# A four-layer graph network: ScalarE takes the filter's first dense layer out of its PSUM bank, VectorE adds a turn later, the sort's transposes stand at the turn's end

## What is computed

```python
def ssp(x):
    return jax.nn.softplus(x) - LOG2
f = ssp(edge @ We1 + be1)
f = f @ We2 + be2
msg = xn[edge_index[1]] * f
agg = jax.ops.segment_sum(msg, edge_index[0], num_segments=N)
```

```python
e = jnp.exp(e - seg_max[dst])
denom = jax.ops.segment_sum(e, dst, num_segments=N)
out = jax.ops.segment_sum(h[src] * alpha[:, None], dst, num_segments=N)
```

## Time and profile before

| | us |
|---|---|
| median of 3 runs | 5322.7 |
| lowest, highest | 5319.41, 5327.09 |
| the profiled execution | 5334.7 |
| its span, first to last instruction | 5332.7 |

### The profile page before, as it was taken

How to read it: one execution, slowest core, us unless ns; L and a number is a source line. 1 busy time by engine, 2 the same in 40 slices (tenths; PEclk the granted TensorE clock), 3 DMA queues, 4 the chain that set the end, 5 groups by cost and what they waited for, 6 DMA issues and landing times. The chain is left out here.

```text
span 5332.7 us, 53511 instructions
## 1 busy us (share of the span) xinstructions
PE 2639.6 (49%) x13173; PEld 2222.8 (42%) x13173; DVE 2702.5 (51%) x7382; ACT 1319.8 (25%) x3951; POOL 3391.0 (64%) x3625
## 2 busy tenths in 40 slices
PE   1477777777566654444443544344443243334445
PEld 1355555556455553333333443333333133333333
DVE  2699888888766653333333443333333533333334
ACT  4587666667366650000000210000000000000001
POOL 0677666767222237777777557777777377777773
PEclk8799888889676775555555665555555555555556
DMA  4676666667388872222221122122222322222224
GB/s 74 175 172 167 149 154 152 159 154 171 54 256 256 261 220 53 53 53 53 53 53 52 38 62 53 51 52 53 53 53 52 51 53 53 51 52 53 53 53 50
DMA packets 460042, 516.96 MB, mean 97 GB/s; under 512 B 85627, under 2 KB 358863, under 8 KB 459734
## 3 DMA queue, kind: packets, MB, share of 16 engines
q0 software_dynamic: 131072, 301.89, 23.9%
q1 hardware_dynamic: 325780, 210.91, 14.4%
q10 hardware_dynamic: 2882, 0.70, 0.1%
HBM read 386.68 MB, written 126.50 MB: 96 GB/s over the span
## 5 line engine op out<-in xcount | busy, mean ns | idle before, releaser
L1476 PE MATMUL bank<-arena 128*128 128x128 f32 x4992 | 1277.0, 438 | 1951.7 <-DVE arena L873 1663.3
L1551 POOL DMA_INDIRECT arena<-node_table,pick x1664 | 1589.4, 955 | 650.8 <-issue 506.9
L1476 PEld LDWEIGHTS bank<-arena 128*128 128x128 f32 x4992 | 1111.3, 328 | 2117.1 <-DVE arena L873 1847.5
L861 DVE TENSOR_TENSOR acc<-acc,bank 128x128 f32 x2496 | 720.4, 289 | 2081.5 <-PE bank L1476 1790.8
L1551 POOL DMA_INDIRECT arena<-gat_table,pick x832 | 850.3, 1022 | 357.7 <-issue 235.0
L1551 POOL DMA_INDIRECT arena<-message_table,pick x832 | 788.7, 948 | 255.8 <-issue 253.2
L1169 ACT COPY xt<-bank 128x512 f32<-128x512 f32 (+1 forms) x39 | 21.6, 554 | 2115.2 <-PE bank L1428 2115.2
L873 DVE TENSOR_TENSOR arena<-iota_free,local 128x512 f32<-128x512 f32 x624 | 428.2, 687 | 3.8 <-issue 2.5
L1465 PE MATMUL bank<-arena 128*128 x1664 | 324.7, 367 | 202.6 <-DVE arena L902 198.6
L1465 PEld LDWEIGHTS bank<-arena 128*128 128x128 f32 x1664 | 293.0, 270 | 234.3 <-issue 233.4
L1630 POOL DMA_DIRECT2D message_table<-arena x208 | 112.8, 542 | 393.1 <-DVE arena L902 389.4
(11 more groups left out here) (215 smaller groups left out, 3167.7 us busy)
## 6 DMA issues: line engine op xcount, KB each, us to landing
arena<-filter_table SPq DMA_DIRECT2D x832, 64.0 KB, 3.2
message_table<-arena POOLq DMA_DIRECT2D x208, 256.0 KB, 3.5
filter_table<-arena SPq DMA_DIRECT2D x196, 256.0 KB
xt<-edge_cols SPq DMA_DIRECT2D x131, 256.0 KB, 3.0
arena<-local_rows SPq DMA_DIRECT2D x208, 128.0 KB
arena<-local_rows POOLq DMA_DIRECT2D x52, 512.0 KB, 5.9
arena<-node_table,pick POOLq DMA_INDIRECT x1664
arena<-edge_cols SPq DMA_DIRECT2D x65, 256.0 KB
```

What stands on the lines that cost most here:

```text
L861: e.tensor_tensor(a, a, bank[6 + t % 2][:, s * P:(s + 1) * P], ALU.add).then_inc(sums, 1)
L1476: ins = e.matmul(bank[6 + n % 2][:, s * P:(s + 1) * P], hot[n % 2][:, s, :], gathered[:, slot(n, s), 0:D], start=True, stop=True)
L1551: e.indirect_dma_start(out=dst, out_offset=None, in_=table, in_offset=bass.IndirectOffsetOnAxis(ap=index, axis=0)).then_inc(done, 16)
```

## The change

ScalarE now reads `bank[0]` twice, right after each other: Abs into `magn` as before, and Relu with the same bias into `edge_t[u % 4]`, the buffer from which the matmul has just read its edges. Then `bank[0]` is free (new semaphore f_taken), and f_hidden_of waits on that and no longer on f_plus. VectorE's f_plus_of becomes a sum of two SBUF tiles and moves one turn later, to lag 4, and from behind the weave to its last piece, so that it stands in the first round. f_filter and f_made_of follow at lags 5 and 6, the store at lag 7. The edge ring has four buffers, its load waits on f_plus. The softplus is split: f_front (Abs, Relu), then gat_weigh, then f_back (Exp, Ln).

The order within the turn changes too: on TensorE, ScalarE and SyncE the background now comes last and not first. A transposition takes two steps, one for each group of four transposes. A second background step comes each fourth turn. So the sort's list is 14 steps longer (238 in place of 224 on VectorE), and the seven window gathers move from GpSimd's turn 179 to 183. The rest are trims without a place in the loop: two rows of weights lie in the gather ring until the ring is used, one constant column, one semaphore and one wait are gone, the arena is larger.

```diff
 def background_turns(t):
-    return (1, 1 + (t % 5 == 0))
+    return (1, 1 + (t % 4 == 0))
...
             def f_plus_of(u):
                 e.wait_ge(f_log, u + 1)
-                e.scalar_tensor_tensor(magn[u % 2][:, :], bank[0][:, :], neg_col["L1_gnn_be1"][:, 0:1],
-                                       magn[u % 2][:, :], ALU.max, ALU.add).then_inc(f_plus, 1)
+                e.tensor_tensor(magn[u % 2][:, :], magn[u % 2][:, :], edge_t[u % 4][:, :], ALU.add).then_inc(f_plus, 1)
...
+                if 0 <= t - 4 < FTICKS:
+                    pieces.append(f_plus_of(t - 4))
                 weave(pieces, background, background_turns(t))
-                if 0 <= t - 3 < FTICKS:
-                    run(f_plus_of(t - 3))
...
+            def f_front(u):
+                e.wait_ge(f_hidden, u + 1)
+                if u > 1:
+                    e.wait_ge(f_done, u - 1)
+                own(e.activation(magn[u % 2][:, :], bank[0][:, :], ACT.Abs, bias=cols["L1_gnn_be1"][:, 0:1]))
+                e.activation(edge_t[u % 4][:, :], bank[0][:, :], ACT.Relu, bias=cols["L1_gnn_be1"][:, 0:1]
+                             ).then_inc(f_taken, 1)
+
+            def f_back(u):
+                m = magn[u % 2][:, :]
+                e.wait_ge(f_taken, u + 1)
+                q = own(e.activation(m, m, ACT.Exp, scale=-1.0))
+                e.wait_ge(own.sem, q)
+                e.activation(m, m, ACT.Ln, bias=1.0).then_inc(f_log, 1)
...
             for t in range(TICKS + 13):
-                weave([], background, background_turns(t))
+                for lag, fn in ((6, f_made_of), (3, f_front), (10, gat_weigh), (3, f_back)):
+                    if 0 <= t - lag < (TICKS if fn is gat_weigh else FTICKS):
+                        fn(t - lag)
                 for lag, fn in ((4, gat_dst), (9, gat_weight)):
                     if (t - lag) % GT == 0 and 0 <= t - lag < TICKS:
                         fn((t - lag) // GT)
-                for lag, fn in ((5, f_made_of), (10, gat_weigh), (3, f_soft)):
-                    if 0 <= t - lag < (TICKS if fn is gat_weigh else FTICKS):
-                        fn(t - lag)
+                weave([], background, background_turns(t))
...
             def f_hidden_of(u):
-                e.wait_ge(edge_in[u % 3], 16 * (u // 3 + 1))
+                e.wait_ge(edge_in[u % 4], 16 * (u // 4 + 1))
                 if u:
-                    e.wait_ge(f_plus, u)
+                    e.wait_ge(f_taken, u)
```

More of the change, by code:

```diff
@@ L171, in build_program @@
         mats = {name: sb("w_" + name, [P, D]) for name in MATS}
-        rows = {name: sb("r_" + name, [P, D]) for name in ROWS}
+        rows = {name: sb("r_" + name, [P, D]) for name in ROWS[2:]}
         cols = {name: sb("c_" + name, [P, 1]) for name in COLS}
@@ L252, in build_program @@
         gat_w, att_prod = gathered[:, 4, :], gathered[:, 5, 0:D]
+        rows.update({name: gathered[:, 6 + k, 0:D] for k, name in enumerate(ROWS[:2])})
         order_row, order_col, order_index, order_src = (
@@ L309, in build_program @@
         ring = [sem(f"ring{k}") for k in range(RT)]
-        sync_in = [sem(f"sync_in{k}") for k in range(6)]
-        edge_in, local_row_in, f_in = sync_in[0:3], sync_in[3:6], sync_in
-        f_hidden, f_log, f_plus, f_done, f_made = (
-            sem("filter_" + n) for n in ("hidden", "log", "plus", "done", "made"))
+        sync_in = [sem(f"sync_in{k}") for k in range(7)]
+        edge_in, local_row_in, f_in = sync_in[0:4], sync_in[4:7], sync_in[0:FT]
+        f_hidden, f_taken, f_log, f_plus, f_done, f_made = (
+            sem("filter_" + n) for n in ("hidden", "taken", "log", "plus", "done", "made"))
         f_out = [sem(f"filter_out{k}") for k in range(2)]
@@ L335, in build_program @@
                                      "x", "xturned", "xkept", "third", "rows"))
-        table_out = [sem(f"table{k}_out") for k in (1, 2)]
+        table_out = sem("table_out")
         plain_hot, plain_product, plain_summed = sem("plain_hot"), sem("plain_product"), sem("plain_summed")
@@ L590, in vector @@
                     e.sem_clear(f_log)
-                    e.scalar_tensor_tensor(magn[0][:, 0:P], bank[0][:, P:2 * P], neg_col["L1_gnn_be1"][:, 0:1],
-                                           magn[0][:, 0:P], ALU.max, ALU.add).then_inc(f_plus, 1)
+                    e.tensor_tensor(magn[0][:, 0:P], magn[0][:, 0:P], magn[1][:, 0:P], ALU.add).then_inc(f_plus, 1)
                     e.wait_ge(f_done, 1)
@@ L1019, in sort_keys @@
                             n += 1
+                            if not h:
+                                yield
                     cur = 1 - cur
@@ L1394, in f_hidden_of @@
             def f_hidden_of(u):
-                e.wait_ge(edge_in[u % 3], 16 * (u // 3 + 1))
+                e.wait_ge(edge_in[u % 4], 16 * (u // 4 + 1))
                 if u:
-                    e.wait_ge(f_plus, u)
-                e.matmul(bank[0][:, :], mats["L1_gnn_We1"][:, :], edge_t[u % 3][:, :], start=True, stop=True
+                    e.wait_ge(f_taken, u)
+                e.matmul(bank[0][:, :], mats["L1_gnn_We1"][:, :], edge_t[u % 4][:, :], start=True, stop=True
                          ).then_inc(f_hidden, 1)
@@ L1573, in second_list @@
                 for kind, _ in PLAN:
-                    if kind == "flip":
+                    if kind != "pair":
                         yield
@@ L1717, in sync @@
             background = [iter(()), second_list()]
-            for t in range(TICKS + 6):
-                weave([], background, background_turns(t))
+            for t in range(TICKS + 7):
                 if t < TICKS:
                     places_in(t)
-                if 0 <= t - 1 < FTICKS:
-                    edges_in(t - 1)
-                if 0 <= t - 6 < FTICKS:
-                    filters_out(t - 6)
+                if t < FTICKS:
+                    edges_in(t)
+                if 0 <= t - 7 < FTICKS:
+                    filters_out(t - 7)
+                weave([], background, background_turns(t))
             for g in background:
```

59 lines of the change are left out of this document (31 added, 28 removed).

## The result

The changed kernel takes 5447.24 us (median of 4 runs, 5434.27 to 5457.15); the kernel before, beside it, 5324.9 (4 runs, 5319.41 to 5338.7). The ratio is 1.0217, 95% interval 1.0196 to 1.0239. The prediction was 5262 with a range of 5235 to 5300, faster with a chance of 0.89. It was wrong in sign: 122 us were lost where 61 were to be gained. The profiled execution took 5457.15 us with a span of 5455.1, against 5334.7 and 5332.7, so the two traces, 122 us apart as well, show the whole difference.

A forecast was written before the change was run, and what follows sets the result against it. VectorE's work and waits were taken to bound the first layer, GpSimd closely behind. Earlier windows (-43), fewer turns of gathers (-20.6) and the tail (+2) gave -62, taken as -61: 5262 us, range 5235 to 5300.

The forecast's parts named there:

- Waits that go: VectorE's waits in the first layer for Ln, mask and a copy, 67.5 us, go, covered by slack between engines.
- the line on DMAs: SP's DMAs keep their count, are issued a turn ahead of use and hide under it; nothing counted for them.
- The rest: First layer's tail costs +2 us; SP's DMAs stay hidden; trims 0; everything behind the first layer moves as a block.
- What bounds the kernel before: First layer, 273 to 1192.7 us: VectorE's 5.46 us of own work a turn plus waits through other engines; GpSimd second.
- f_plus itself: On VectorE, 157 f_plus go from 745 ns to about 685 as sums of two SBUF tiles: -9.4 us.
- GpSimd's pace: Gathers lengthened by VectorE's SBUF reads, 0.110 us each, make turns of 5.44 us, so window gathers start at 1150 us.
- ScalarE: A new 0.68 us Relu in each of 196 turns costs 3 us, in the counting turns; nothing counted before 273 us.
- Fewer turns of gathers behind the windows: Window gathers come four turns later, leaving four turns of GpSimd's gathers fewer after them: -20.6 us.
- Later windows: GpSimd bounds from the window gathers on at 5.15 us a turn; they come four turns later, adding about 17.2 us before.
- The waits only move: VectorE waits for masks or products behind TensorE at half clock; two thirds of 67.5 us return: 5307 us; chance 0.07.
- The port chain: One gather a turn waits out VectorE's run of five instructions; GpSimd at 6.2 us a turn, 5383 us; chance 0.10.
- The 0.05 for slower: Chance that the whole kernel turns slower, taken from half of the port chain's 0.10.

The follow-up runs named there:

- the same four kernels: The changed kernel; with a third magn buffer; with SyncE's filter store ahead of the edge load; with both edits: 5453.86, 5400.38, 5399.2, 5304.11 us.
- the kernel with both fixes: The changed kernel with a third magn buffer and the filter's store ahead of the load of edges on SyncE; 5304.11 us, ratio 0.9941.
- the run that adds the load alone: The kernel before with one more ScalarE Relu of bank[0] into a spare tile in each filter turn, result unused; 5347.98 us, ratio 1.0028.
- with the store first: The changed kernel, two magn buffers, ScalarE's weights ahead of Abs, the filter's store ahead of SyncE's edge load; 5315.11 us, ratio 0.9965.
- with f_plus behind the sums: The kernel with both fixes, with f_plus put behind the last sum of VectorE's turn at the same lag; 5303.62 us, ratio 0.9942.
- the third-buffer kernel: The changed kernel with a third magn buffer only; 5952.98 us, ratio 0.9958 on the slow chip, 5400.38 us, ratio 1.0121 on a usual one.

## Why the prediction was wrong

The step that failed is the cover of *Waits that go*, together with the line on DMAs in *The rest*: both put at nothing the waits that the new lags and the load's new wait make. The runs showed two circles there, worth 150 us together.

**What bounds the kernel before**: nothing speaks against it. VectorE's work in the stretch is unchanged (805 us in turns that now last longer), and f_plus waited for the Ln until the change.

**Waits that go**: the first half of the step holds (60.1 us to 2.9, ScalarE's idle before transposes gone). What failed is its cover, "a slack of most of a turn between every two engines". It was counted for the edges that the change draws anew: Ln to f_plus, Relu to the hidden matmul, transposes to the exchange. The edges that the change shortens without touching their line were not counted. By the same slip the prediction says of ScalarE that "nothing waits on it within the same turn any more": the filter waits for its copy of the same turn, 273 us in all. The filter went from lag 4 to 5 and ScalarE's Abs stayed at 3; with two magnitude buffers the distance 5 - 3 is just the number of buffers, so reader and writer of a buffer meet in the same turn. Its price: from 5453.86 to 5400.38 with the other circle there, from 5399.2 to 5304.11 without it, 53 to 95 us.

**"DMAs on SP keep their count, are issued a turn ahead of use and hide under it"** failed too. The store keeps its count and its distance, but it stands behind a load whose wait moved from a matmul of an earlier turn to VectorE's f_plus of the same turn. The prediction named no one queued behind that wait. Price: 55 to 96 us by the same four kernels.

**f_plus itself**, -9.4 us: right, 686 and 683 ns against 685 expected.

**GpSimd's pace**, 5.44 us a turn: of the right kind and a little small. In the kernel with both fixes a turn is (1174.8 - 264) / 163 = 5.59 us. By its row the gathers take 1.073 us with 0.305 between them, 5.51 us for four, and 15.1 us of waiting for products is 0.09 a turn. Against the forecast's 0.110 us of lengthening it is 0.13. The term missed by 0.15 x 163 = 24 us, about half of it longer gathers and half the waits for products. Fewer turns of gathers behind the windows gave 134.3 us in place of 152.9, -18.6 and not -20.6. So the first layer of this kernel ends 40.4 us earlier than before and not 62; by the medians the whole kernel gains 31. The 9 us between the two can't be placed: the stages behind the first layer differ by up to 42 us among the traces of the usual chips.

**ScalarE**, +3 us: 16 in the run that adds the load alone. That the counting turns had "nothing idle" holds for the turn shown; by the earlier trace rows Abs waited 11.3 us for the hidden matmul in 29 of them. Nothing was counted before 273 us, where the changed kernel lost 21.3 us.

**Later windows** in the changed kernel: its last 24 turns run at (1462.7 - 1302.8 - 8.7) / 24 = 6.3 us with seven window gathers of 1.24 us off, not at GpSimd's 5.15. The pair of waits of the first circle is there too: from 1311 to 1462 us the filter waits 34.3 us for the copy, Abs 27.2 for the filter.

**The rivals.** "The waits only move" came nearest in what VectorE shows, idle before its maximum, but it was priced at two thirds of 67.5 us and put down to TensorE's clock, which did not move (0.90 in both). A rival that replaces a wait can cost more than the wait; it was wrong to cap it. The port chain, the one slower case, was not it: it needed 6.2 us a turn by gathers alone, 6.2 / 4 - 0.305 = 1.245 us each, and they take 1.074 in the changed kernel. The 0.05 for slower left out the whole class of cases that happened.

## What to carry to other kernels

When a stage is moved by a turn, list for every buffer its writer and its next reader with their lags, and subtract: a distance equal to the number of buffers means both stand in one turn, and then their places in the lists decide. Do the same for every semaphore wait in an in-order queue, and ask which unrelated transfer stands behind it. Where a repair gives half of what was expected, look for a second circle of nearly the same length before giving up on the first: here 53 and 55 us alone were 150 together. And before adding a buffer, see whether work of the waiting engine can be put into the wait; with the store first, that came to within 11 us of the time with a third buffer (14 us, if each is taken against the kernel before of its chip).

## What the runs showed of the hardware

**A gather waits to the end of a VectorE instruction with two SBUF inputs, and sometimes of the whole run.** In the kernel with both fixes, GpSimd and VectorE around 281 us and around 446 us:

```profile
280.40 0.69 DVE L760 TENSOR_TENSOR arena<-arena,xt 128x512 f32<-128x512 f32 x1
280.53 1.37 POOL L1571 DMA_INDIRECT arena<-gat_table,pick  x1 [0.30 <-issue]
281.00 0.68 DVE L416 TENSOR_TENSOR arena<-arena 128x512 f32<-128x512 f32 x1
281.61 0.69 DVE L417 TENSOR_TENSOR arena<-arena 128x512 f32<-128x512 f32 x1
```

```profile
444.95 0.69 DVE L760 TENSOR_TENSOR arena<-arena,xt 128x512 f32<-128x512 f32 x1
445.08 2.57 POOL L1571 DMA_INDIRECT arena<-gat_table,pick  x1 [0.30 <-issue]
445.55 0.69 DVE L416 TENSOR_TENSOR arena<-arena 128x512 f32<-128x512 f32 x1
446.15 0.69 DVE L417 TENSOR_TENSOR arena<-arena 128x512 f32<-128x512 f32 x1
```

Both gathers start 0.13 us into f_plus with the same run behind it. The first ends at 281.90, 0.81 us behind the end of f_plus (281.09), the second at 447.65, 0.81 us behind the end of the whole run (446.84); an undisturbed gather takes 0.94. Counted over the trace from 273 to 1140 us, 113 gathers longer than 1 us met a run of two or three such instructions and ended so behind one of them: 83 behind the first, 30 behind the last. What decides between the two is not shown. The longest gather is 2.74 us, and with f_plus behind the sums, where runs are mostly shorter, it is 1.98.

Two SBUF inputs are what holds: in the kernel before, the 66 gathers that start while f_plus reads its bank and one SBUF tile take 0.94 us in the mean and 0.95 at most; in the changed kernel, the 51 that start while the sum of two SBUF tiles runs take 1.69. The Trainium skill ("SBUF — State Buffer", Who interferes with whom) says that a VectorE instruction with two SBUF inputs contends with a GpSimd instruction that reads SBUF, and the traces agree. Where it tells how long the shared ports are held, it speaks of one instruction; 83 of the 113 gathers agree, the other 30 don't.

**One chip was 12% slower as a whole.** The kernel before takes 5977.76 us there. In the trace of the third-buffer kernel on that chip 4415 us pass behind the first layer, 3938 in that of the kernel before on the usual one, where the change touches only trims. VectorE waits there in another way: its largest wait between 2200 and 5200 us, first of the third-buffer kernel on that chip, then of the kernel before on the usual one.

```profile
DVE acc L862 <- remote: 1446.4, 182, 20.2
```

```profile
DVE acc L861 <- PE bank L1476: 1616.1, 567, 10.4
```

On that chip the profile puts most of the idle time down to a releaser outside of the core's records, in pieces of up to 20 us. What it is was not tried. On it the third buffer alone is faster than before, on the usual chip it is slower. So a ratio to a base on the same chip is the least that is needed, and here not even its sign carried over to the other chip.
